# The outputs at a batch's end: division ahead of one low part, and the middle bank scaled by ScalarE and added by GpSimd

## The reference

```
f = x @ Wq + bq ;  g = x @ Wk + bk ;  h = x @ Wv + bv      # x: 4 x 1024 x 128
beta = softmax(f @ g.T)                                    # 1024 x 1024 for each image
out = gamma * (beta @ h) + x
```

## Time and profile before

| | us |
|---|---|
| median of the runs (3) | 406.61 |
| lowest, highest | 405.34, 406.91 |
| the profiled execution, its time | 399.32 |
| its span | 397.5 |
| TensorE busy in it | 351.2 (88%) |
| VectorE busy | 301.9 (76%) |
| ScalarE busy | 271.4 (68%) |
| GpSimd busy | 270.9 (68%) |

### The profile page before, as it was taken

The page is one execution under the profiler, slowest core; times in us unless marked ns, Lnnn a source line. Parts: engine busy times, 40 slices in busy tenths (PEclk is TensorE's granted clock), DMA queues, the critical chain, the costliest instruction groups (busy, mean ns, idle before and its releaser), DMA issues.

```text
span 397.5 us, 12541 instructions
## 1 busy us (share of the span) xinstructions
PE 351.2 (88%) x4900; PEld 228.8 (58%) x4900; DVE 301.9 (76%) x830; ACT 271.4 (68%) x435; POOL 270.9 (68%) x322
## 2 busy tenths in 40 slices
PE   2668999998999999998979899999998989989693
PEld 0335665565555666666656456654674856657373
DVE  6758888887888888889677677787668797784424
ACT  3466888886877788887835644455478877868481
POOL 7477966667777777798776786756257785868421
PEclk9999999999999999999899999999999999999799
DMA  5701100111111000010000000000010011010102
GB/s 181 253 20 28 30 24 22 27 28 30 27 31 31 26 26 26 26 30 15 2 3 2 15 13 2 2 2 0 2 29 14 15 51 31 2 55 2 53 2 58
DMA packets 15597, 12.29 MB, mean 31 GB/s; under 512 B 3992, under 2 KB 14137, under 8 KB 15545
## 3 DMA queue, kind: packets, MB, share of 16 engines
q1 hardware_dynamic: 14208, 11.03, 9.5%
q10 hardware_dynamic: 1336, 0.54, 0.5%
HBM read 4.22 MB, written 2.10 MB: 16 GB/s over the span
## 4 chain that ended last, share of the span: by engine, by line
PE 61%; DVE 16%; ACT 6%; issue 5%; DMA 5%; SPq 3%; POOL 2%; ACTq 0%; DVEq 0%; POOLq 0%
PE ps L359 8%; PE ps L1577 7%; PE ps L911 6%; PE ps L939 5%; PE ps L993 4%; PE ps L932 4%; DMA k_t<-qk_t 4%; PE ps L920 3%; PE ps L901 3%; SPq L871 3%; PE ps L379 3%; DVE ob L1701 2%; PE ps L903 2%; DVE mx L1670 2%; PE ps L1419 2%
## 5 line engine op out<-in xcount | busy, mean ns | idle before, releaser
L1752 POOL TENSOR_TENSOR el<-e,eh 128x1024 f16<-128x1024 f32 x28 | 59.6, 2131 | 31.1 <-ACT eh L1744 30.8
L1297 POOL TENSOR_TENSOR p_lo<-e_buf,p_hi 128x1024 f16<-128x1024 f32 x32 | 68.2, 2130 | 5.6 <-ACT p_hi L1153 3.8
L1289 POOL TENSOR_TENSOR rot<-ta,tb 128x256 f32<-128x256 f32 x32 | 23.3, 728 | 39.1 <-DVE tb L1084 38.3
L359 PE MATMUL ps<-y_t,fc_w 128*128 128x512 f16 x192 | 46.2, 380 | 2.8 <-DVE y_t L582 1.2
L1111 DVE TENSOR_REDUCE ps<-ps 128x16 f32<-128x1024 f32 x32 | 39.4, 1232 | 8.0 <-PE ps L920 7.2
L911 PE MATMUL ps<-mask,identb 128*128 128x512 bf16 x128 | 39.9, 394 | 6.4 <-DMA k_t<-qk_t 6.2
L1735 ACT ACTIVATE e<-ps 128x1024 f32<-128x1024 f32 x32 | 32.6, 1020 | 18.5 <-PE ps L1566 18.1
L1577 PE MATMUL ps<-val,eh 128*128 128x129 f16 x512 | 38.6, 226 | 7.5 <-DVE ob L1701 6.9
L1223 ACT ACTIVATE e_buf<-ps 128x1024 f32<-128x1024 f32 x32 | 32.7, 1023 | 15.6 <-PE ps L932 15.4
L1577 PEld LDWEIGHTS ps<-val,eh 128*128 128x128 f16 x512 | 32.5, 100 | 18.4 <-issue 11.0
L288 POOL TENSOR_TENSOR hl<-hid,hh 128x512 f16<-128x512 f32 x24 | 27.7, 1159 | 19.7 <-DVE yn L569 10.5
(11 more groups left out here) (164 smaller groups left out, 986.4 us busy)
## 6 DMA issues: line engine op xcount, KB each, us to landing
k_t<-qk_t SPq DMA_DIRECT2D x126, 32.0 KB, 1.9
x_all<-in_x SPq DMA_DIRECT2D x8, 256.0 KB, 4.5
out<-ob SPq DMA_DIRECT2D x8, 192.0 KB, 2.1
yr<-xr SPq DMA_DIRECT2D x16, 64.0 KB, 2.0
mask_f<-in_mask SPq DMA_DIRECT2D x1, 512.0 KB, 3.6
fc_w<-in_fc_w SPq DMA_DIRECT2D x1, 512.0 KB, 5.4
out<-ob SPq DMA_DIRECT2D x4, 128.0 KB, 1.9
fc_w<-in_fc_w SPq DMA_DIRECT2D x1, 256.0 KB, 5.3
```

The lines of the kernel that those rows point to most:

```text
L359: last = pe.matmul(ps[:, bank, :], fc1_w16[:, ws, 128 * block_:128 * block_ + 128], y_t[:, v, ys, :], start=(n == 0), stop=(n == 2))
L1297: pool.tensor_tensor(p_lo[:, u], e_buf[:, u], p_hi[:, u], ALU.subtract).then_inc(plo_done, 1)
L1752: pool.tensor_tensor(el[:, T % H_BUFS, :], e4[:, T % E_BUFS, :], eh[:, T % H_BUFS, :], ALU.subtract).then_inc(el_done, 1)
```

## The change

Three things change, all in the last stage, at the end of a batch.

1. `finish` is split. `factors_of` holds the division and `rg`; what stays in `finish` are the products. The order on VectorE becomes: factors of bank 0, factors of bank 1, products of bank 0, factors of bank 2, products of bank 2. The wait for the bank before (`o_ready`) in front of each division is gone.
2. Bank 1's products leave VectorE. ScalarE multiplies each of its three blocks by its column of `rg` into a new buffer `fin` (three instructions, between exp and eh of the step), and GpSimd adds x to all three in one instruction, ahead of its low part of that step. TensorE waits for `fin` before it writes bank 1 again, SyncE waits for GpSimd's addition before it stores bank 1.
3. On VectorE all of this now stands ahead of the step's low part. Only one step of those with a `finish` has one on VectorE: T = 25.

```diff
@@ values, on TensorE
                     for j in range(3):
                         if m == 0:
-                            wait(pe, o_ready, 3 * (b - 1) + j + 1)
+                            if j == 1:
+                                wait(pe, fin_done, b)
+                            else:
+                                wait(pe, o_ready, 2 * (b - 1) + j // 2 + 1 if b else 0)
@@ on VectorE
-            def finish(b, j):
-
-                u, n = b % 2, blocks(j)
+            def factors_of(b, j):
+
+                n = blocks(j)
                 if j < 2:
                     dve.wait_ge(pvb_done, 2 * b + j + 1)
                 else:
                     dve.wait_ge(pv4_done, b * BT + BT)
-                wait(dve, o_ready, 3 * b + j)
                 dve.reciprocal(pv4[:, j, 0:len(n), DIM], pv4[:, j, 0:len(n), DIM]).then_inc(den_done, 1)
                 dve.wait_ge(den_done, 3 * b + j + 1)
                 dve.tensor_scalar(rg[:, n[0]:n[-1] + 1], pv4[:, j, 0:len(n), DIM], cols[:, 1:2], None, ALU.mult)\
                     .then_inc(rec4_done, 1)
+
+            def finish(b, j):
+
+                u, n = b % 2, blocks(j)
                 if j == 0:
                     dve.wait_ge(x2_shifted, 2 * b + 2)
                     if b >= 2:
                         dve.wait_ge(stored[u], 48)
-                dve.wait_ge(rec4_done, 3 * b + j + 1)
+                dve.wait_ge(rec4_done, 3 * b + max(j, 1) + 1)
...
+                if n == 1 and b >= 1:
+                    factors_of(b - 1, 0)
+                    factors_of(b - 1, 1)
+                    finish(b - 1, 0)
+                    factors_of(b - 1, 2)
+                    finish(b - 1, 2)
                 if b < B:
                     if by_vector(T):
...
-                if n == 1 and b >= 1:
-                    for j in range(3):
-                        finish(b - 1, j)
@@ on ScalarE
+            def scaled_outputs(b):
+
+                act.wait_ge(rec4_done, 3 * b + 2)
+                wait(act, o_fin, b)
+                for i, k in enumerate(blocks(1)):
+                    last = act.activation(fin[:, i, :], pv4[:, 1, i, 0:DIM], ACT.Copy, scale=rg[:, k:k + 1])
+                last.then_inc(fin_done, 1)
+
...
+                if n == 1 and b >= 1:
+                    scaled_outputs(b - 1)
...
+            scaled_outputs(B - 1)
@@ on GpSimd
+            def outputs(b):
+
+                pool.wait_ge(x2_shifted, 2 * b + 2)
+                if b >= 2:
+                    pool.wait_ge(stored[b % 2], 48)
+                pool.wait_ge(fin_done, b + 1)
+                n = blocks(1)
+                pool.tensor_tensor(ob[:, b % 2, n[0]:n[-1] + 1, :], fin[:],
+                                   x_all[:, b * BT + n[0]:b * BT + n[-1] + 1, :], ALU.add).then_inc(o_fin, 1)
+
             for T in range(TILES):
+                if T % BT == 1 and T > BT:
+                    outputs(T // BT - 1)
...
+            outputs(B - 1)
@@ store, on SyncE
-                    sp.wait_ge(o_ready, 3 * b + j + 1)
+                    if j == 1:
+                        sp.wait_ge(o_fin, b + 1)
+                    else:
+                        sp.wait_ge(o_ready, 2 * b + j // 2 + 1)
```

More of the change, by code:

```diff
@@ L1369, in build @@
         o_ready = sem("o_ready")
+        fin_done = sem("fin_done")
+        o_fin = sem("o_fin")
         stored = [sem(f"stored{u}") for u in range(2)]
@@ L1388, in build @@
         rg = sb("rg", [128, BT])
+        fin = sb("fin", [128, 3, DIM])
         ob = sb("ob", [128, 2, BT, DIM])
```

## The result

| | before | after |
|---|---|---|
| median, first comparison (5 runs each) | 405.34 us | 391.55 us |
| ratio, 95% interval | | 0.974 (0.970 to 0.978) |
| compared again (6 runs of after) | 404.03 | 393.25, ratio 0.977 (0.972 to 0.981) |
| compared a third time (6 runs of after) | 403.46 | 392.04, ratio 0.974 (0.969 to 0.978) |
| mean of all runs of the later comparisons (87) and of all of the kernel after (19) | 403.7 | 393.3 |

A forecast was written before the change was run, and what follows sets the result against it. It took TensorE, idle or slowly clocked while waiting for VectorE's outputs at batch ends, as the bound. Terms of 1.0 + 1.1 + 5.2 + 0.4 = 7.7 us off a 406.6 median gave 398.9 us, range 395.8 to 401.8.

The forecast's parts named there:

- I take 7.7 off it: Whole kernel: the summed gain of 7.7 us subtracted from the shown runs' median of 406.6, giving 398.9.
- term 1: First batch end of the last stage: the next projection, and all behind it, comes 1.0 us earlier.
- term 2: Second batch end: bank 2 is free sooner, so scores 19 start 1.1 us earlier.
- term 3: Third batch end: outputs precede the low part and the clock stays up; exp of tile 31 comes 5.2 us earlier.
- term 4: Program's end: the last store goes out at 394.6 in place of 395.00, 0.4 us gained.
- ScalarE gives ends 0 and 1 back: First two batch ends: ScalarE's added work cancels their gains; 5.6 us gained, 401.0; chance 0.10.
- The clock falls at end 2 all the same: Third batch end: TensorE's clock still drops; gain there 3.3 in place of 5.2, so 400.8; chance 0.06.
- Slower: All three batch ends: the clock falls, costing 0.9 us more than the gain, 407.5; chance 0.03.
- More: First two batch ends: the runs' extra time is clock falls that shorter waits prevent; 6.7 us more, 392.2; chance 0.07.
- both clock rivals: Clock still falls at the third batch end (400.8, chance 0.06), or at all three (407.5, chance 0.03).

The follow-up runs named there:

- e13: Kernel after, with five reductions on VectorE behind the last store, to make it about as long as before: 398.94 us.
- e2: Kernel before, with only the outputs moved ahead of VectorE's low part: 399.22 us, ratio 0.990.
- e6: Kernel before, with twelve spare matmuls on TensorE where it waits at the third batch end: 400.78 us, ratio 0.994.
- e8: Kernel after, with bank 1's division behind bank 0's products again: 398.72 us, ratio 0.989.
- e3: Kernel before, with only bank 1's division ahead of bank 0's products, all products still on VectorE: 399.64 us, ratio 0.991.
- e9: Kernel before, with twelve spare matmuls at the third batch end and four ahead of each wait for banks 1 and 2 at the others: 402.17 us, ratio 0.999.
- e7: Kernel after, with ScalarE's scaled copies behind eh of the step in place of ahead of it: 392.66 us, ratio 0.975.
- e4: Kernel before, with early division and outputs ahead of the low part, all products still on VectorE: 393.99 us, ratio 0.978.
- e16_look: Kernel before, unchanged, one more profile to count clock falls: 94.31 us from first to last exp.
- e11_look: Kernel before, unchanged, one more profile to place its low clock: 90.47 us from first to last exp.
- e12_look_after: Kernel after, unchanged, one more profile to place its low clock: 84.45 us from first to last exp.

## Why the prediction was wrong

The direction, the mechanism and, to 0.2 us, each term of the stage were right; the forecast time was not. By the first median the error is 7.4 us (398.9 against 391.55); by the means, which rest on more runs, it is 5.6 (398.9 against 393.3) and has two halves: the base, 2.9 (406.6 against 403.7), and the gain, 2.7 (7.7 against 10.4). That the sum on the profile, 399.3 less 7.7 = 391.6, meets the first median is luck: the profiled execution had 11 us of low clock where the mean run of before has 19.

**The step that failed** is "I take 7.7 off it", with the sentence ahead of it that no row says why the runs lie 7.3 above the profile. It moved a sum made on one quiet execution onto another base as if both kernels carried the same extra time. The gain from falls other than end 2's was thereby put at nothing in the sum. The runs showed otherwise. A straight line through the 87 runs of before gives 0.38 us of time for each us of low clock, from 396.6 with none to 403.7 at the mean of 18.9; through the 19 of after, 0.35, from 390.5 to 393.3 at 8.1. So the gain of 10.4 is 6.1 at no low clock and 4.3 from the clock. The first is drawn out beyond the runs (none of before has under 9.5 us of low clock), and the split is an estimate. The prediction's sum held 5.8 of the first (7.7 less the clock's 1.9 at end 2), which was near, and 1.9 of the second.

**End 0, term 1** (1.0): measured 1.18. The scaled copies took 0.88 in place of 0.95 (0.367 each, where 0.384 was taken), and eh overlapped their end by 0.1, which I had not taken off: eh starts 1.58 behind the first division where 1.74 was forecast. That is nearly all of the difference. By the Trainium skill, "ScalarE: Activation LUTs", section "What ACT_TABLE_LOAD costs", three such copies with two overlaps would take 0.97 (an estimate from its figures); the trace has 0.88, and the measurement decides. The wait of TensorE for bank 1 was over in time, as said.

**End 1, term 2** (1.1): measured 1.26, scores 19 start 3.61 behind the division in place of 3.77, for the same reason. GpSimd's addition took 1.00, as forecast. The cover for the low part of tile 17 held: GpSimd has it at 352.84 (350.71 and 2.13 for one of the three) and TensorE takes it at 353.19, 0.35 later, where 0.5 was forecast.

**End 2, term 3** (5.2): measured 5.35. TensorE resumes at 370.39, 2.12 behind the first division, and ScalarE paces from there at 2.0 per tile. The clock stayed up, in all six profiles of the kernel after (e13's among them). e2 gives the shares: moving the outputs alone brings 4.0 of it, and e6 shows 1.7 for the fall alone where 1.9 had been worked out (more where end 1 fell before it, by 0.4 to 0.8).

**The program's end, term 4** (0.4): the last store's issue ends 8.21 behind the last exp (389.22 to 381.01) and ended 8.71 behind it (395.37 to 386.66): 0.5. From that issue's end to the end of the span it is 2.1 to 3.9 us, varying from profile to profile in both kernels, which hides it in a single pair.

**The rivals.** "ScalarE gives ends 0 and 1 back" was false, and e8 shows what would have made it true. "The clock falls at end 2 all the same" and "Slower" were false. "More" (0.07 in the forecast, 392.2) was right at end 1 for 1.2 of the 6.7 us that it named, and its number was close by luck, off a base 2.9 too high: end 1 falls in four of seven profiles of before and costs 1.5 at once (24.2 to 24.3 against 22.73), 1.9 to 2.3 with what follows, on average over the seven 1.2; in the six of after there is none. End 0 never fell: tiles 8 to 15 took 24.31 or 24.32 in all seven. The prediction had held against both clock rivals that the matmuls behind waits of 0.67 and 0.66 us run at the full clock; that was true of the one profile, and behind the same waits at end 1 the clock fell in four of seven.

**What adds up.** 7.8 in the stage, 0.5 at the end and 1.2 for end 1 make 9.5 of 10.4 (of 10.0 without the longest runs). The remaining 0.9 us has no place. The falls at the stage's start (two of seven before, one of six after, 1.66 each) and in the part ahead of it (0 to 14 us of low clock, in both) come in code that the change doesn't touch; their mean can't be told apart with so few profiles. The difference of the means is itself known to about 1 us only (twice its standard error), so the remainder may be nothing. Its cause stays open. That the length of the execution does it is excluded (e13). The low clock of the kernels orders as before 18.9, e3 15.3, e9 13.7, e8 12.9, e2 12.0, e6 10.9, after 8.1, e7 7.6, e4 7.1: those with both the move and the early division lie lowest. That shorter waits at ends 0 and 1 take away more low clock than these few profiles caught would fit this, but it is argued from means, not shown in a trace.

## What to carry to other kernels

Don't take a gain worked out in one profile off the median of other runs before asking what the runs hold that the profile doesn't: where the mean granted clock of the runs is known, it tells; here it is 19 us of low clock against 11 in the profile shown (for the three runs that the prediction had, it was not known). Where TensorE waits in several short pieces at a place that repeats, count the place as a possible fall of the clock even if the profile at hand has none there, and give its removal a part of that price. When work is handed to a neighbour engine, advance what it needs first: here one division ahead of three products, worth 2.8 us of stage with the hand-over (e8) and 1.1 without it (e4 against e2). In this kernel that alone decided whether the hand-over was hidden.

## What the runs showed of the hardware

- The same instructions with the same waits, to 0.01 us, ran with and without a fall of the granted clock: e16_look and e11_look at end 1, e6 and e9 at end 2, tiles 0 to 7 of after in e12_look_after (24.5) and in the other profiles (22.83). The stretches at 1.2 GHz lasted 3.4 or 6.8 us and cost 1.5 to 2.3 us each in the stage; at end 1 and in e9 they began behind two waits of TensorE of 0.67 to 0.94 us with half a us of matmuls between them, not behind a long one. The Trainium skill, "TensorE: Matmul & The Clock Gate", section "What's actually happening", says that the gate judges by a free-running window that doesn't start with the kernel. These pairs agree, in that equal work met it differently; they don't show the window itself.
- Spare matmuls in a wait don't hold the clock reliably: with twelve of them at end 2 it stayed up in e6's profile and fell in e9's.
- Three ACTIVATEs of 128 columns out of PSUM, with a tensor as scale, took 0.88 us together, 0.367 each; GpSimd's addition of 128x384 took 1.00.
